# Two-layer perceiver on one core: second attention in groups of four positions on two column halves, with a reordered beginning

## The reference

```python
q = x @ Wq                                  # 16 heads of 64
k, v = split(context @ Wkv)
mask = j_idx % n_q == i_idx                 # n_q = 64 positions, 1024 keys
sim = where(mask, einsum('bhid,bhjd->bhij', q, k) * scale, max_neg)
out = einsum('bhij,bhjd->bhid', softmax(sim), v) @ Wout + bout
```

## Time and profile before

| | |
|---|---|
| median of 3 runs | 895.59 us (895.39 to 897.55) |
| the profiled execution | 890.92 us, its span 889.1 |
| PE busy | 833.7 us (94%), 7892 records |
| DVE busy | 515.6 us (58%) |
| ACT busy | 422.0 us (47%) |
| POOL busy | 105.6 us (12%) |
| DMA | 128.13 MB, mean 144 GB/s |
| second attention, 652.0 to 725.3 | PE busy 67.06 us of 73.30 |

### The profile page before, as it was taken

The page is one execution under the profiler, slowest core; times in us unless marked ns, Lnnn a source line. Parts: engine busy times, 40 slices in busy tenths (PEclk is TensorE's granted clock), DMA queues, the critical chain, the costliest instruction groups (busy, mean ns, idle before and its releaser), DMA issues.

```text
span 889.1 us, 20080 instructions
## 1 busy us (share of the span) xinstructions
PE 833.7 (94%) x7892; PEld 675.1 (76%) x7892; DVE 515.6 (58%) x1216; ACT 422.0 (47%) x854; POOL 105.6 (12%) x102
## 2 busy tenths in 40 slices
PE   5999999999889798999999999999989999779997
PEld 3788788888757696888888888886369967568885
DVE  4778878788645656555555555554345632675332
ACT  3657576676652224445455444443465642432221
POOL 2333312340000530000000000000011000400200
PEclk9999999999999899999999999999999999989999
DMA  7446644575090000113213303004516668113970
GB/s 294 188 161 214 237 175 154 167 260 202 2 393 9 3 4 2 59 83 142 87 56 142 115 27 142 0 0 172 206 48 230 243 234 346 83 44 150 366 300 25
DMA packets 25867, 128.13 MB, mean 144 GB/s; under 512 B 2360, under 2 KB 8272, under 8 KB 21712
## 3 DMA queue, kind: packets, MB, share of 16 engines
q1 hardware_dynamic: 24624, 111.51, 33.8%
q0 software_dynamic: 1184, 15.77, 4.4%
HBM read 126.75 MB, written 0.52 MB: 143 GB/s over the span
## 4 chain that ended last, share of the span: by engine, by line
PE 79%; DVE 10%; DMA 5%; issue 3%; ACT 2%; SPq 1%; DVEq 0%; ACTq 0%
PE PS L459 13%; PE PS L460 12%; PE PS L461 12%; PE PS L778 4%; DMA arena<-in_bias 3%; PE PS L1223 3%; PE PS L899 3%; PE PS L1024 3%; PE PS L1235 3%; PE PS L790 3%; PE PS L1043 3%; PE PS L767 3%; PE PS L479 2%; PE PS L1012 2%; PE PS L997 2%
## 5 line engine op out<-in xcount | busy, mean ns | idle before, releaser
L1405 ACT CAST w_h<-arena 128x768 fp32r<-128x768 f32 x64 | 53.4, 836 | 124.7 <-PE PS L461 124.7
L1756 DVE TENSOR_TENSOR w_l<-arena,w_h 128x768 fp32r<-128x768 f32 x64 | 61.2, 958 | 87.1 <-ACT w_h L1405 87.0
L459 PE MATMUL PS<-xnT_h,w_h 128*128 128x512 f32 x256 | 99.7, 390 | 1.4 <-DVE xnT_l L453 1.4
L460 PE MATMUL PS<-xnT_l,w_h 128*128 128x512 f32 x256 | 99.6, 389 | 0.0
L461 PE MATMUL PS<-xnT_h,w_l 128*128 128x512 f32 x256 | 99.6, 389 | 0.0
L1605 DVE CUSTOM_DVE_ANT_0 arena<-PS,arena 128x512 f32<-128x512 f32 x128 | 86.9, 715 | 19.8 <-PE PS L767 17.8
L1303 ACT ACTIVATE arena<-arena 128x1024 f32<-128x1024 f32 x64 | 73.5, 1151 | 11.1 <-DVE arena L1605 11.1
L778 PE MATMUL PS<-consts,arena 128*128 128x128 f32 x512 | 68.3, 277 | 0.7 <-ACT arena L1308 0.4
L778 PEld LDWEIGHTS PS<-consts,arena 128*128 128x128 f32 x512 | 55.9, 141 | 10.6 <-issue 3.6
L1763 DVE TENSOR_TENSOR arena<-PS,arena 128x512 f32<-128x512 f32 x64 | 44.3, 692 | 29.1 <-PE PS L461 27.3
L459 PEld LDWEIGHTS PS<-xnT_h,w_h 128*128 128x128 f32 x256 | 48.0, 188 | 11.7 <-DVE xnT_l L453 1.8
(11 more groups left out here) (313 smaller groups left out, 1774.7 us busy)
## 6 DMA issues: line engine op xcount, KB each, us to landing
arena<-in_bias SPq DMA_DIRECT2D x64, 512.0 KB, 4.1
arena<-in_wall SPq DMA_DIRECT2D x8, 3072.0 KB, 10.1
arena<-in_wf SPq DMA_DIRECT2D x8, 2052.0 KB, 12.2
hT<-in_ctxT SPq DMA_DIRECT2D x12, 1024.0 KB, 6.6
arena<-in_ctxT SPq DMA_DIRECT2D x4, 1024.0 KB, 6.6
arena<-in_ctxG SPq DMA_DIRECT2D x4, 1024.0 KB, 5.3
hT<-in_ctxG SPq DMA_DIRECT2D x4, 1024.0 KB, 5.1
arena<-in_w SPq DMA_DIRECT2D x2, 1024.0 KB, 6.1
```

The source lines that it names most:

```text
L459: pe.matmul(out, a[0], b[0], start=start, stop=False)
L460: pe.matmul(out, a[0], b[1], start=False, stop=False)
L1405: act.copy(w_h[:, s % 4, :], stage[s // 8 % 2][:, s % 8, :]).then_inc(sem("c_wh"), 1)
L1756: dve.tensor_tensor(w_l[:, s % 4, :], stage[s // 8 % 2][:, s % 8, :], wide(w_h[:, s % 4, :]), ALU.subtract).then_inc(sem("c_wl"), 1)
```

## The change

The positions are taken in sixteen groups of four (`QI = 4`, `QS = 16`). A group has 64 rows (16 heads x 4) and 64 keys. Two groups lie on top of each other in the partitions, group 2g in 0 to 63 and 2g+1 in 64 to 127, so the scores are written by two column halves of TensorE, and Z (scores and probabilities) has 64 columns a pair. Each probability half is transposed in its own quadrant, the first by a transpose, the second by a plain matmul with the identity; ScalarE copies out the first (64 partitions), VectorE the second. They land on the diagonal blocks of `PTx`, whose other blocks GpSimd sets to zero once; the sums stay 16 matmuls of 128x128. U is stored by groups when it is copied from the queries, `U[half][batch x group, head x 4 positions]`, so nothing regroups it; the results are written back as whole runs, and the value matmuls read it with a stride. The context comes in a new order (`ctxD`), of the same size. In TensorE's list the transposes of b stand between the two halves of the scores of b+1; the scores of the first two batches stand ahead, then eight `warm` matmuls; four more stand before the last transposes. The loops over batches of this stage are written out.

At the beginning SyncE loads only the 298 columns of constants that the first stage needs, then wk, the context, wq, wv; GpSimd loads the other constants after its loop of the first attention. TensorE starts with 16 matmuls of 128 columns on zeros. VectorE copies both halves of the transposed tokens and takes over the second half of the context's low part; the wv parts come later.

```diff
-GRP, GI = 8, 8
+QI = 4
+QS = S // QI
+GRP = QS // 2
...
-    U = cd(KC, XH, TOK)
+    U = [cd(B * QS, XH * QI) for _ in range(KC)]
...
-            sp.dma_start(consts[:], A["consts"]).then_inc(sem("in_const"), 16)
+            sp.dma_start(consts[:, 0:FIRST], A["consts"][:, 0:FIRST]).then_inc(sem("in_const"), 16)
...
+            for b in range(B):
+                if b >= 2:
+                    sp.wait_ge(sem("d_sim"), 2 * (b - 1))
+                sp.dma_start(ctxT1[b % 2], A["ctxD"][b].rearrange("(k p) n -> p k n", p=P))\
+                  .then_inc(sem(f"d_ctxT{b % 2}"), 16)
+                if b >= 2:
+                    sp.wait_ge(sem("d_w"), 4 * (b - 1))
+                sp.dma_start(ctxG[b % 2], A["ctxG"][b]).then_inc(sem(f"d_ctxG{b % 2}"), 16)
...
+            pe.wait_ge(sem("c_zero"), 1)
+            for _ in range(16):
+                pe.matmul(PS[:, 7, 0:P], zero8, zero8, start=True, stop=True)
+            pe.wait_ge(sem("in_const"), 32)
...
+            def sims(b, hf):
...
+                if b:
+                    pe.wait_ge(sem("d_z"), 2 * (b - 1) + hf + 1)
+                for g in range(4 * hf, 4 * hf + 4):
+                    for dc in range(KC):
+                        for n, r in enumerate(halves):
+                            q = 2 * g + n
+                            last = pe.matmul(PS[r, hf, (g % 4) * 64:(g % 4 + 1) * 64], U[dc][:, b * QS + q, :],
+                                             ctxT1[b % 2][:, dc, q * 64:(q + 1) * 64], start=dc == 0, stop=dc == KC - 1)
...
+            def turned(b):
...
+                    for g in range(4):
+                        pe.transpose(PS[0:S, 2 + hf, g * 64:(g + 1) * 64], Z[0:S, hf, g, :], C("ident")[0:S, 0:S])
+                        last = pe.matmul(PS[S:P, 2 + hf, g * 64:(g + 1) * 64], Z[S:P, hf, g, :], C("ident")[S:P, S:P],
+                                         start=True, stop=True)
...
+            for b in range(2):
+                for hf in range(2):
+                    sims(b, hf)
+            warm(pe, 7, 8)
+            for b in range(B):
+                if 0 < b < B - 1:
+                    sims(b + 1, 0)
+                if b == B - 1:
+                    warm(pe, 0, 4)
+                turned(b)
+                if 0 < b < B - 1:
+                    sims(b + 1, 1)
+                sums(b)
...
-                                         U[:, ki, 2 * c + h2, :], start=ki == 0, stop=ki == KC - 1)
+                                         U[ki][:, :, QI * (2 * c + h2):QI * (2 * c + h2 + 1)], start=ki == 0, stop=ki == KC - 1)
...
-                    dve.tensor_copy(U[:, 0, 2 * c + h2, :], bank(2 + 2 * h2)).then_inc(sem("d_ue0"), 1)
+                    dve.tensor_copy(U[0][:, :, QI * (2 * c + h2):QI * (2 * c + h2 + 1)],
+                                    bank(2 + 2 * h2).rearrange("p (q i) -> p q i", i=QI)).then_inc(sem("d_ue0"), 1)
```

More of the change, by code:

```diff
@@ L46, in const_layout @@
         "half2": ((p % 32) // DK == np.arange(2)[None, :]),
[L47 removed]
+        "group": np.where(p % QI == np.arange(64)[None, :] % QI, 0.0, -BIG),
         "upper": i > j,
@@ L1030, in sums @@
-            def sums(i, j):
-                b = i * 2 + j
-                for hf in range(2):
[L1033 to L1039, removed]
+            def sims(b, hf):
+                pe.wait_ge(sem(f"d_ctxT{b % 2}"), b // 2 * 16 + 16)
+                if b:
[6 more added lines that the diff above has]
+                                             ctxT1[b % 2][:, dc, q * 64:(q + 1) * 64], start=dc == 0, stop=dc == KC - 1)
+                last.then_inc(sem("d_sim"), 1)
@@ L1040, in sums @@
+            def sums(b):
+                pe.wait_ge(sem(f"d_ctxG{b % 2}"), b // 2 * 16 + 16)
+                for hf in range(2):
+                    for n in range(2):
+                        pe.wait_ge(sem(f"d_te{n}"), 2 * b + hf + 1)
                     for dc in range(KC):
-                        pe.wait_ge(sem(f"d_we{dc}"), b * 2 + hf + 1)
+                        if b:
+                            pe.wait_ge(sem(f"d_we{dc}"), 2 * (b - 1) + hf + 1)
                         for g in range(4):
@@ L1055, in _ @@
-            sims(B // 2 - 1, 1)
-            sums(B // 2 - 1, 0)
-            sums(B // 2 - 1, 1)
+            for dc in range(KC):
+                pe.wait_ge(sem(f"d_ue{dc}"), 2 * FC)
+            for b in range(2):
[11 more added lines that the diff above has]
+                sums(b)
@@ new lines, in scores @@
+            def scores(b, hf):
+                dve.wait_ge(sem("d_sim"), 2 * b + hf + 1)
+                if b:
+                    dve.wait_ge(sem("d_t"), 2 * (b - 1) + hf + 1)
+                for g in range(4):
+                    last = dve.tensor_tensor_reduce(out=Z[:, hf, g, :], in0=PS[:, hf, g * 64:(g + 1) * 64],
+                                                    in1=C("group"), scale=-1.0, scalar=3e38, op0=ALU.add,
+                                                    op1=ALU.min, accum_out=mx1[:, hf, g:g + 1])
+                last.then_inc(sem("d_z"), 1)
@@ L1826, in _ @@
-            scores(0)
-            grouped(1)
-            probabilities(0)
-            with dve.Fori(1, B - 1) as b:
-                ch.enter(b - 1, 2)
-                scores(b)
-                grouped(b + 1)
+                    dve.wait_ge(sem("d_w"), 4 * b + 2 * hf + 1)
+                    dve.tensor_copy(U[0][:, b * QS + 8 * hf:b * QS + 8 * hf + 8, :].rearrange("p q n -> p (q n)"),
+                                    bank(4 + 2 * hf)).then_inc(sem("d_we0"), 1)
+            for hf in range(2):
+                scores(0, hf)
@@ L1833, in _ @@
+            probabilities(0)
+            dve.wait_ge(sem("d_set"), 1)
+            for b in range(1, B):
+                scores(b, 0)
+                turned(b - 1)
+                scores(b, 1)
                 probabilities(b)
                 summed(b - 1)
-                ch.leave(B - 2)
-            scores(B - 1)
-            probabilities(B - 1)
-            summed(B - 2)
+            turned(B - 1)
             summed(B - 1)
```

169 lines of the change are left out of this document (56 added, 113 removed).

## The result

The changed kernel takes **911.04 us** (median of 4 runs, 908.34 to 913.03) beside 896.55 for the kernel before (4 runs, 895.39 to 897.55): a ratio of 1.0153, 95% interval 1.0122 to 1.0183. It is 1.5% slower where 1.6% faster was forecast; 881.6 and the range up to 889.5 are missed by far, on rival (f)'s side.

The account below looks back on a forecast made before the run. TensorE was taken as the bound, busy 833.7 of 889.1 us, with transfers late next. Second attention -11.1 and beginning -2.9 sum to -14.0: 876.9 profiled, 881.6 with the 4.7 to the median carried; range 876.0 to 889.5.

Parts of the forecast that it names:

- rival (f): Second attention: transposes and matmuls on the two quadrants wait for each other's end, turning 3.9 a batch, 903.6 us; chance 0.04.
- 16 of them are 1.05: Second attention's turning: eight transposes and eight plain 64x64 matmuls a batch, priced from L936 at 0.066 each, taken as 0.94 us.
- only the transpose mode is new: Argument against rival (f): L936 already overlaps plain matmuls on opposite quadrants, so the turning differs only in its transposes.
- turning point: Gain turns to loss where the turning takes 2.0 more than 0.94, about 2.9 us a batch.
- the 1.8 of the transfers: Second attention: time the forecast included for late context transfers; without them binding, 1.8 us better.
- forecast gain of 14.0: Whole kernel: 11.1 us less by the second attention and 2.9 less by the beginning.
- D: Second attention: time from the end of a batch's sums, when context transfers are issued, to their landing; taken as 7.4 us.
- rival (b): Second attention: each transfer pair as slow as the first, D = 8.6, end 3.6 us later, 885.2 us; chance 0.10.
- rival (e): Second attention: column halves of the scores do not overlap, 1.7 us more a batch, 893.4 us; chance 0.03.
- the shape changes: Second attention, TensorE: tile shapes change four times a batch, 0 to 0.15 us each, taken as 0.1, 0.4 a batch.
- rival (d): Runs of 4 elements cost: L1066 twice as long, +14.0, 895.6 us, or its copies slower; chance 0.06.
- before 10.3: Beginning: wq, queued behind the context on SyncE, was to land before 10.3 us, when the token copies end.

Follow-up runs that it names:

- e2: Changed kernel with plain matmuls against the identity in both quadrants of the turning, no transposes: 888.91 us, ratio to before 0.9915.
- e1: Changed kernel with each half's turning ordered as four transposes, then four plain matmuls, instead of by turns: 889.6 us, ratio to before 0.9932.
- e5: e2 with SyncE issuing ctxD right behind the scores that free its buffer, ahead of ctxG of the batch before: 881.68 us, ratio to before 0.9837.
- e3: Kernel before with only the reordered beginning (zero matmuls, load order, late constants, half of ctx_l on VectorE): 893.23 us beside 896.54.
- e10: e5 without the warming matmuls and with GpSimd's indirect expert transfers issued behind the dense group: 874.27 us, ratio to before 0.9753.
- e12: e10 plus six more zero matmuls at the beginning, in the wait for wq: 871.44 us, ratio to before 0.9740.

## Why the prediction was wrong

In the profiled executions the forecast was 876.9 and 908.34 came, 31.4 more.

- **The step that failed: "16 of them are 1.05, and half of them have one record instead of two, so 0.94; the bounds are 0.85 and 1.3."** It measured 3.43. The price was taken from L936, which alternates quadrants but never the operation; e2 shows that this price is right for plain matmuls, e1 that each change to or from a transpose costs about 0.12 and that the quadrants then don't overlap. 8 x (3.42 - 0.94) = 19.8 us. (The 0.94 does not follow from its own words either, 24 records of 32 would be 0.79; next to 3.43 that is nothing.) The upper bound was no bound: "only the transpose mode is new" was the reason to look for a far one. Rival (f) had the right side and named the alternation; its price of 3.9 came from starts to ends and was a little high, its chance of 0.04 far too low. Its turning point, 2.9 us a batch, was passed: the turning alone, 19.8 less the 1.8 of the transfers, outweighs the forecast gain of 14.0 by about 4 us, an estimate from these terms.
- **A term that was missing: the clock.** Nothing in the sum or the rivals let it fall in this stage. In the changed kernel, on the chain, the second halves of the scores lost 3.6, the sums 4.8, the turning 0.6: 9.0 us.
- **The transfers** did not bind in the changed kernel, since a batch took 10.9 ((728.65 - 663.49) / 6) and hid them; that takes back the 1.8 which the forecast had for them. 19.8 + 9.0 - 1.8 = 27.0, and L1061 starts at 738.34 where 714.2 - 2.9 = 711.3 was forecast. In e1 and e2 they did bind, as the step said, but D, from the end of the sums to the landing, was 8.5 to 8.8 in e1 (678.33 to 686.87, for one) instead of 7.4, close to rival (b)'s 8.6.
- **The remaining 4.4 us** lie behind this stage: in the last stage the pauses, absent from the one profile of before, make it 4.6 longer. Because the forecast carried over the 4.7 us between that profile and the median, they are in 881.6 already; that distance was noted, and not asked about.
- **Right:** column halves that overlap (scores at 1.08 a half with their share of the shape changes, rival (e) out); the shape changes nearly so (e5's period of 7.04 less 1.87 scores, 1.05 turning and 3.57 sums leaves 0.55, where 0.4 was taken); the sums and L1061 in runs of 4 unchanged, 13.97, and the copies of the queries in runs of 4 at 1.29 for two (rival (d) out); no other engine late. The beginning gave 3.3 in e3 where 2.9 was forecast.
- **The beginning in the changed kernel itself:** wq landed later than "before 10.3", and after 1.97 us of waiting for it the clock fell for 3.4 us, so first scores at 20.29 and not 17.9. The second attention's scores still start at 648.56, where 651.3 - 2.9 = 648.4 was forecast; part of that is luck, since this start moved from 652.24 to 650.92 between two executions of the kernel before. The timeline of the changed kernel:

```profile
10.98 5.40 PE L694 MATMUL PS<-xnT,arena 128*128 128x512 f32 x8 [1.97 <-DMA arena<-in_wq]
20.29 0.51 PE L753 MATMUL PS<-kT_h,qz_h 32*128 32x512 f32 x4 [1.16 <-DVE kT_l L1561]
```

With the turning as forecast and ctxD issued earlier (e5) the whole change takes 881.68 and L1074 starts at 712.49. That e5 lands on the forecast of 881.6 is in part chance, since it contains the earlier issue, which the forecast did not have. Without it (e2) the time is 888.91, at the upper end of the range.

## What to carry to other kernels

Take the price of small operations from a row with the same sequence of operations, not only the same shape: a transpose between plain matmuls is a sequence of its own, and grouping by kind, or a plain matmul against the identity, cost nothing here and were worth over 20 us by the medians. When a stage gets cheaper, look at once at what its transfers wait for: the queue's order held them back by one wait that was not theirs. And if the one profiled execution stands 0.5% away from the median, profile a second one before reading it.

## What the runs showed of the hardware

- A change between a transpose and a plain matmul, both in 64x64 tiles on opposite quadrants, costs about 0.12 us; a pair by turns takes 0.43 us, two plain matmuls on the two quadrants 0.13 (changed kernel, e1, e2).
- The clock fell with TensorE busy without a gap: 20.4 us at half clock in the alternating order, none in this stage in the grouped order (e1). Two executions of one kernel can differ in this too: none against 6.8 us in this stage of the kernel before.
- In the changed kernel, e1, e2 and e5 two column halves with all rows each keep 0.058 to 0.068 us a matmul of 64 columns, group changes included, and a record of it 0.029, where a record of 128 columns on the whole array takes 0.112. The Trainium skill (TensorE: Matmul & The Clock Gate, Part 3) lets weight loads overlap only between different row groups; the rows go against it.
- With indirect transfers issued by GpSimd in the middle of a dense group of 64-column matmuls, TensorE paused in four groups a run, at the same records in all 11 traces that have pauses: six stops of some 0.36 us and shorter ones, 4.8 us in all. Issued behind the group they stopped nothing (e10, e12). One profiled execution, the first of the kernel before, had no such pauses in spite of the early issue.
